# Projection weights made bf16 by eight DRAM-to-DRAM casting DMAs from GpSimd, in place of ScalarE copies

## What is computed

```
ln_out = LN(layernorm(x))
q, k, v, qx = per-head LN of fp8(ln_out / in_scale) @ w      # kx, vx from ctx_2048
core = attention(q, k, v);  xout = attention(qx, kx, vx)
catq = fp8(concat(core, xout) / proj_smooth)
x = x + (catq @ wproj.T) * (proj_in_scale * proj_w_scale)
g = silu(z @ Wgate.T) * (z @ Wup.T);  x = x + g @ Wdown.T    # z = layernorm(x), W = (int - 128) * scale
```

## Time and profile before

| | |
|---|---|
| median of 3 runs | 1793.88 us (1792.93 to 1796.43) |
| the profiled execution's own time | 1795.76 us |
| its span, first to last instruction | 1793.9 us |
| PE busy | 1675.9 us, 93% |
| ACT busy | 1399.3 us, 78% |
| DVE busy | 1364.5 us, 76% |
| POOL busy | 1138.4 us, 63% |
| granted TensorE clock, mean | 0.977 of full |

### The profile page before, as it was taken

One profiled execution on the slowest core, in us unless ns is written; L12 is line 12 of the kernel. 1 busy time (PEld: TensorE's weight loads), 2 busy tenths in 40 slices (PEclk: granted clock), 3 DMA queues, 4 the chain that ended last, 5 costly groups with the idle time before them and its releaser, 6 DMA issues.

```text
span 1793.9 us, 44172 instructions
## 1 busy us (share of the span) xinstructions
PE 1675.9 (93%) x15776; PEld 1230.4 (69%) x15776; DVE 1364.5 (76%) x3181; ACT 1399.3 (78%) x2944; POOL 1138.4 (63%) x1043
## 2 busy tenths in 40 slices
PE   1449999999999999999999999999999979999999
PEld 1437778878887887788788877787888534444444
DVE  8969888997998799889979987997777652323232
ACT  6888999999999999999999999999999622121211
POOL 1137788778788877887787788778877613030202
PEclk9669999999999999999999999999999989999999
DMA  5557799888888988888798878888999970112100
GB/s 183 177 190 125 147 159 166 147 148 161 153 157 144 172 152 148 160 161 148 148 166 152 151 151 176 146 148 172 176 196 205 196 229 0 67 74 98 42 24 24
DMA packets 671666, 257.41 MB, mean 143 GB/s; under 512 B 616288, under 2 KB 634976, under 8 KB 671456
## 3 DMA queue, kind: packets, MB, share of 16 engines
q1 hardware_dynamic: 671456, 254.71, 71.0%
HBM read 74.10 MB, written 29.51 MB: 58 GB/s over the span
## 4 chain that ended last, share of the span: by engine, by line
ACT 28%; PE 21%; DVE 19%; POOL 15%; issue 10%; SPq 4%; DMA 3%; ACTq 0%; DVEq 0%; POOLq 0%
POOL local L1129 10%; ACT local L1041 7%; ACT local L1038 7%; ACT local L961 5%; PE ps_s L727 5%; DVE w_raw L1199 4%; ACT local L948 3%; DVE local L1371 2%; POOL w_raw L1113 2%; SPq L614 2%; DVE sq_sum L1284 2%; PE ps_pj L844 2%; PE ps_pj L845 2%; PE ps_o L844 2%; PE ps_o L845 2%
## 5 line engine op out<-in xcount | busy, mean ns | idle before, releaser
L1129 POOL TENSOR_TENSOR local<-local 128x512 bf16<-128x512 f32 x512 | 594.0, 1160 | 258.6 <-ACT local L1041 258.2
L720 PE MATMUL ps_pj<-wide 128*128 128x256 bf16 (+1 forms) x5544 | 584.9, 255 | 6.7 <-DVE wide L1208 4.0
L720 PEld LDWEIGHTS ps_pj<-wide 128*128 128x128 bf16 x5544 | 468.8, 98 | 116.8 <-ACT local L961 7.5
L1038 ACT ACTIVATE local<-ps_s,neg_max 128x512 f32<-128x512 f32 x512 | 380.5, 743 | 33.5 <-DVE neg_max L1363 30.4
L767 PE MATMUL ps_o<-v_hi,local 128*128 128x129 bf16 x2048 | 375.7, 221 | 7.6 <-DMA local<-local 5.6
L1041 ACT ACTIVATE local<-ps_s,neg_max 128x512 bf16<-128x512 f32 x512 | 382.5, 747 | 0.0
L769 PE MATMUL ps_o<-v_hi,local 128*128 128x129 bf16 x2048 | 375.3, 219 | 0.0
L768 PE MATMUL ps_o<-local 128*128 128x128 bf16 x2048 | 375.1, 218 | 0.0
L1363 DVE TENSOR_REDUCE neg_max<-ps_s 128x1 f32<-128x512 f32 x512 | 344.7, 673 | 37.2 <-PE ps_s L787 36.4
L961 ACT ACTIVATE local<-ps_pj,head_rstd 128x128 f32<-128x128 f32 x756 | 234.3, 416 | 51.6 <-issue 50.5
L1099 POOL TENSOR_TENSOR head_rstd<-sq_sum,minus_half 128x3 f32<-128x3 f32 x256 | 241.9, 945 | 27.3 <-DVE sq_sum L1284 27.3
(11 more groups left out here) (119 smaller groups left out, 2673.5 us busy)
## 6 DMA issues: line engine op xcount, KB each, us to landing
quantised_heads<-local SPq DMA_DIRECT2D x128, 128.0 KB, 2.5
w_raw<-w_group SPq DMA_DIRECT2D x56, 256.0 KB, 3.2
wide<-quantised_heads SPq DMA_DIRECT2D x3, 4096.0 KB, 13.1
local<-local SPq DMA_TRANSPOSE x640, 3.2
wide<-packed_weights SPq DMA_DIRECT2D x32, 256.0 KB, 3.2
wide<-x SPq DMA_DIRECT2D x7, 1024.0 KB, 8.6
w_raw<-w_proj SPq DMA_DIRECT2D x10, 512.0 KB, 4.5
wide<-quantised_heads SPq DMA_DIRECT2D x16, 256.0 KB, 3.4
```

Source lines behind the costliest of these rows:

```text
L720: last = mm(dst[:, at:at + n], lhs, w_at(par, part, c, cross * 512 + at, n), start=(k == 0), stop=(k == len(terms) - 1))
L1038: a(p_exp[:, u % 2], ps_s[u % 2][:], ACT.Exp, bias=neg_max[:, u % 4:u % 4 + 1])
L1129: tt_(pp[:, u % PP_BUFS, 1], p_exp[:, u % 2], pp[:, u % PP_BUFS, 0], ALU.subtract)\
```

## The change

The 16 copies of `w_proj` pieces on ScalarE, with their 16 loads and 16 stores on SP, go. In their place GpSimd issues eight DMAs, behind its last `power`/`shift` pair of the opening and ahead of `head_power(0)`. Each reads 128 x 4 x 512 floats of `w_proj` in DRAM (1024 KB) and writes as many bf16 to `packed` (512 KB), each with a semaphore of its own. The 17th piece, of `w_down`, still goes the old way, but earlier: loaded into `heads_t`, copied by ScalarE ahead of `weight_scale(2)`, stored by SP behind the loads of `ctx`. SP's first loads of the next weights wait no more for the pieces' stores; it waits for the last piece's store behind them. The eight casts are waited for before the first `tail_load`, in the last group.

```
-            for i in range(len(OPENING_PIECES)):
-                pre_store(i)
-                if 3 <= i + 2 < len(OPENING_PIECES):
-                    pre_load(i + 2)
-                if i == 4:
-                    load_ctx(3)
-            for i in range(len(OPENING_PIECES) - 3, len(OPENING_PIECES)):
-                sp.wait_ge(pre_out[i % 3], 16 * (i // 3 + 1))
+            last_raw = piece_raw(PIECES - 1, heads_t.rearrange("p h t -> p (h t)"))
+            sp.dma_start(last_raw, weight_piece(PIECES - 1)[0]).then_inc(last_in, 16)
+            for b in range(1, B):
+                load_ctx(b)
+            sp.wait_ge(last_made, 1)
+            at = weight_piece(PIECES - 1)[1]
+            sp.dma_start(packed[:, at:at + piece_size(PIECES - 1)],
+                         heads_t.rearrange("p h t -> p (h t)")[:, 0:piece_size(PIECES - 1)]).then_inc(last_out, 16)
...
+            sp.wait_ge(last_out, 16)
...
                 if n == 0:
+                    for landed in (*cast_out, last_out):
+                        sp.wait_ge(landed, 16)
...
+            act.wait_ge(last_in, 16)
+            src, _, offset = weight_piece(PIECES - 1)
+            kept = heads_t.rearrange("p h t -> p (h t)")
+            a(kept[:, 0:piece_size(PIECES - 1)].rearrange("p (r w) -> p r w", w=src.shape[2]),
+              piece_raw(PIECES - 1, kept), ACT.Copy, bias=offset).then_inc(last_made, 1)
             weight_scale(2)
...
-                for n in range(max(2 * i - 1, 0), 2 * i + 1):
-                    pack(n)
             head_norm(TILES - 1, TILES - 1, 0)
             ctx_part(2)
-            for n in range(2 * TILES - 1, len(OPENING_PIECES)):
-                pack(n)
...
+            for n in range(CASTS):
+                rows = slice(CAST_ROWS * n, CAST_ROWS * (n + 1))
+                nc.gpsimd.dma_start(packed[:, 0:GU_AT].rearrange("p (f n) -> p f n", n=DM)[:, rows],
+                                    w_proj.rearrange("(f p) n -> p f n", p=P)[:, rows]).then_inc(cast_out[n], 16)
 
             for i in range(TILES):
                 head_power(i, i)
```

More of the change, by code:

```diff
@@ L57 @@
 QUANT_STEPS = 4
+CASTS = 8
 COLS = {}
@@ L285, in block_kernel @@
         heads_stored = sem("heads_stored")
-        pre_in = [sem(f"pre_in{i}") for i in range(3)]
-        pre_done = sem("pre_done")
-        pre_out = [sem(f"pre_out{i}") for i in range(3)]
+        last_in = sem("last_in")
+        last_made = sem("last_made")
+        last_out = sem("last_out")
+        cast_out = [sem(f"cast_out{i}") for i in range(CASTS)]
         pack_in = [sem(f"pack_in{i}") for i in range(2)]
@@ L326, in block_kernel @@
         PIECES = WP_PIECES + GU_PIECES + WD_PIECES
-        OPENING_PIECES = [*range(WP_PIECES), PIECES - 1]
+        CAST_ROWS = G * HEADS // CASTS
         GROUP_PIECES = [*range(WP_PIECES, PIECES - 1)]
@@ L330, in block_kernel @@
         PACK = ((39, 43, 47, 0), (49, 51, 55, 0), (53, 59, 63, 1))
-        PRE_LAST = (0, 2, 4, 6, 8, 10, 12, 14)
         SLOTS = B * UNITS
@@ L424, in tile_bank, with pack_buffer @@
             return START_BANKS[i % len(START_BANKS)] if at_start(t) else ps_pj[i % 2]
[L426 to L429, removed]
+        def pack_buffer(i):
+            return w_raw[:, i * GW:(i + 1) * GW].bitcast(BF16)
         def weight_piece(n):
@@ L577, in pack_load @@
                     sp.wait_ge(w_ready, CH * (g + 1) + 4 + W_FREE)
-                sp.dma_start(piece_raw(n, pre_buffer(1 + i)), weight_piece(n)[0]).then_inc(pack_in[i], 16)
+                sp.dma_start(piece_raw(n, pack_buffer(i)), weight_piece(n)[0]).then_inc(pack_in[i], 16)
             def pack_store(g, j):
@@ L583, in pack_store @@
                 sp.wait_ge(pack_done, PER_GROUP * g + j + 1)
-                sp.dma_start(packed[:, at:at + piece_size(n)], pre_buffer(1 + i)[:, 0:piece_size(n)]).then_inc(pack_out[i], 16)
+                sp.dma_start(packed[:, at:at + piece_size(n)], pack_buffer(i)[:, 0:piece_size(n)]).then_inc(pack_out[i], 16)
             def tail_load(n):
@@ L986, in qk_part @@
                 qk_whole(q, j, n)
[L989 to L994, removed]
             for i in range(TILES):
@@ L1112, in pack @@
                 src, _, offset = weight_piece(n)
-                nc.gpsimd.tensor_scalar(pre_buffer(1 + i)[:, 0:piece_size(n)].rearrange("p (r w) -> p r w", w=src.shape[2]),
-                                        piece_raw(n, pre_buffer(1 + i)), offset, None, ALU.add).then_inc(pack_done, 1)
+                nc.gpsimd.tensor_scalar(pack_buffer(i)[:, 0:piece_size(n)].rearrange("p (r w) -> p r w", w=src.shape[2]),
+                                        piece_raw(n, pack_buffer(i)), offset, None, ALU.add).then_inc(pack_done, 1)
+            for n in range(CASTS):
+                rows = slice(CAST_ROWS * n, CAST_ROWS * (n + 1))
+                nc.gpsimd.dma_start(packed[:, 0:GU_AT].rearrange("p (f n) -> p f n", n=DM)[:, rows],
+                                    w_proj.rearrange("(f p) n -> p f n", p=P)[:, rows]).then_inc(cast_out[n], 16)
             for i in range(TILES):
```

## The result

The changed kernel is slower: 1816.95 us (median of 4 runs, 1816.44 to 1819.66) against 1794.36 us for the kernel before in the same runs, a ratio of 1.0124 with a 95% interval of 1.0112 to 1.0137, some 22.6 us. The forecast was 1830 us, 36 later; sign and mechanism held, the size of one term did not.

A forecast was written before the change was run, and what follows sets the result against it. ScalarE, with VectorE close behind, was taken to bound the opening, TensorE the groups. Seven 8.0 us holds put the exponent at 168.4 us, 36.3 later: 1830 us, likeliest case 1809 to 1859, 8-in-10 range 1780 to 1859.

The forecast's parts named there:

- The bound: Opening, 68 to 120 us: ScalarE (busy 46 of 52 us) sets the pace, VectorE (43) close behind; TensorE bounds the groups.
- What is removed: Opening: without ScalarE's copies the first exponent comes at 118.8 us, 13.3 earlier; by ScalarE alone 22.8 us.
- the last chunk: ScalarE's last scaled chunk, which VectorE's last quantise waits for; without the copies forecast at about 106.5 us.
- The tail behind the chunk: ScalarE's fixed work from the last scaled chunk to the first exponent: 17.5 us before, 12.3 without copies and their waits.
- Where the wait ends: Opening: walk from GpSimd's release to the first exponent, forecast 42.6 us behind it.
- R: The moment GpSimd is free for head_power(0): forecast 125.8 us; free of cost until 76.2, break-even at 89.5.
- How often GpSimd is held: GpSimd's queue ahead of head_power(0): seven of the eight DMAs hold it, the eighth costs only its issue, 1 us.
- How long one cast holds it: GpSimd in the opening: each held cast takes 8.0 us, a 4.5 load plus a 3.5 store; range 5.1 to 12.
- That GpSimd isn't held: Rival: GpSimd hands over each DMA in under 1 us, so the 13.3 us are gained: 1780.6 us; chance 0.18.
- That room comes free while a transfer runs: Rival: GpSimd is held at the pace of the bytes, R 99 to 114 us, time 1804 to 1818; chance 0.10.
- Slow casts: Rival: converting makes each cast take more than 12 us, R beyond 154 us, time above 1859; chance 0.08.
- The change does nothing: Rival: the opening's copies were hidden, or gain and hold cancel near 20.7 us; 1790.3 to 1797.5 us, chance 0.03.

The follow-up runs named there:

- two casts: The changed kernel with only the first two of its eight casts made, the rest of the projection weights missing: 1786.19 us, ratio 0.9939 to the kernel before.
- the run with sixteen: The changed kernel with sixteen casts of 2 rows each instead of eight of 4, same bytes: 1803.42 us, ratio 1.0036 to the kernel before.
- plain copy: The changed kernel with its eight DMAs copying float32 to float32 into their own DRAM tensor, projection weights not made: 1819.36 us, ratio 1.0123 to the kernel before.

## Why the prediction was right in sign and too large

**The bound** was read rightly: nothing of the loss or the gain is outside the opening.

**What is removed**: 13.3 us forecast, 12.6 measured at the exponent, with VectorE next, not ScalarE alone (22.8). Without casts the last chunk ended at 106.3 us (106.5 forecast), in part by luck: the last `quantise` was counted at 8.3 us, and its rows before make 9.2 (114.62 to 123.79), while VectorE was done at 117.1 and not at 114.8. The tail behind the chunk took 13.2 us, not 12.3.

**Where the wait ends**: R + 42.6 was forecast, R + 44.4 measured, 1.8 us more, in two halves. The last chunk ends at R + 31.2 and not R + 30.3: VectorE waits 0.91 us for `ctx_part(1)` on ScalarE, as with two casts. And the tail is 13.2 us here too, which was taken as fixed: ScalarE waits 0.84 us in it for the last tile's `head_rstd`, whose `evacuate(7)` stood behind this instruction of VectorE's,

```profile
137.60 3.06 DVE L1242 TENSOR_TENSOR wide<-wide,local 128x4096 bf16<-128x4096 bf16 x1
```

2.29 us in the tiles before. It began while an instruction of GpSimd's was running (136.50 to 138.51). A second of 3.06 us, at 148.13, has no `evacuate` behind it, and the exponent doesn't wait for it.

**How often GpSimd is held**: seven times, none behind the eighth, as forecast. That the room holds one such DMA and not two was my assumption, and no row of before bears on it; the runs showed one cast in flight with 1024 bytes and three with 2048.

**How long one cast holds it** is the term that was mis-sized: 8.0 us forecast, 5.69 measured. Seven times 2.31 is 16.2 us; less the 1.8 us above it is the 14.8 us by which the forecast for the exponent (168.4) was too late, but for 0.4, which are the start of the first cast (68.64, not 68.8) and the issue of the eighth (0.74, not 1). I took a load and a store one after the other, and wrote myself that a cast overlaps them. It does: a cast lands in 5.4 us, where a load and a store of half its bytes take 8.0 one after the other. During the one that begins at 74.55, from 74 to 80 us, the DMA engines move

```profile
q0 software_dynamic: 528, 0.52, 57.6%
...
packed_weights<-w_proj POOLq DMA_DIRECT2D x1, 512.0 KB, 5.3
```

528 packets with 0.52 MB written (a cast is booked by what it writes), in some 3.5 us of the 6. The right row was the load of as many rows, 5.1 us, which I had as the lower end; it is still 0.6 us a cast short. The row nearest in mechanism, one DMA with 512 rows of 2 KB, should have been taken over the one nearest in bytes.

**Rivals.** That GpSimd isn't held (0.18) is out: it idles 4.9 us each time. That room comes free while a transfer runs (0.10): not seen; the fourth half-size cast was written at 73.57 us, 0.3 behind the first's landing. Its sum was also askew: it set reads and writes together (12.6 MB) against a rate, 215 GB/s, that counts a DMA's bytes once (0.52 MB for a cast that reads 1.05). Slow casts (0.08): out, a cast lands in 5.4 us. The change does nothing (0.03): out, 1.0124. VectorE's work beside a DMA's issue would show in the first interval, when VectorE was still busy: 5.91 us against 5.61 in the next, 0.3 us at the most. In other runs it differs: beside two-input ones a half-size cast takes 0.68 us as when alone (70.19 us in the run with sixteen). Beside the one-input ones from 75 us on a full cast takes 1.36 and 1.44 us with twice the room, and the second plain copy 1.76 instead of 0.75. So beside VectorE's work a DMA's issue took 1 us more at the most (1.76 less 0.75). The row that was to show GpSimd beside a two-input instruction of VectorE's, 116.01 us with 2.05, ran beside one-input ones (L1253 at 115.88, L1256 at 117.14).

What stays open is whether other shapes (rows of other lengths, SBUF as the target) hold GpSimd as long, and whether converting costs the DMA engines anything. That the exponent moved by 21.5 us and the median by 22.6 I put down to the scatter of single executions; the 5.5 us by which the time behind the exponent varies over the ten kernels fit that, but it wasn't tried.

## What to carry to other kernels

A DMA that GpSimd issues was not free to its queue here: with 1024 bytes a partition one cast of 512 rows was in flight, and all that stood behind the next on GpSimd waited 4.9 us for its landing. So ask of such DMAs how many the reserved room holds. Give more room (1.0124 to 0.9981 here), cut the DMAs so that several fit (to 1.0036), or put them where GpSimd waits for others anyway; here the last turned a loss of 1.2% into a gain of 0.8% over the kernel before, with the same DMAs. And price a new wait per unit with its break-even first (2.6 us a cast here). Both ends of the hold, 5.1 and 12 us, lay above it, so that its size couldn't turn the sign; what could was whether GpSimd is held at all (0.18 against), which no row showed.

## What the runs showed of the hardware that I had not expected

- A casting DMA from DRAM to DRAM lands as soon as a plain copy of the same 512 rows read: 5.4 us both, with half the bytes written in twice as many packets.
- Three in flight follow each other by 2.5 to 2.9 us, one at a time by 5.7, with the casts' queue at 63.7% (74.5 to 108.5 us).
- Cutting the DMAs in two made the row of them shorter (`head_rstd` at 96.1 for 109.3 us).
- The wait for room has no releaser in the profile: it stands as idle time with "issue" ahead of the next DMA (4.9 us in the changed kernel), which begins 0.3 us behind a landing.
